# Layer 0: 148 score tiles of the maximum pass between the units of the expert network

## The reference, cut to what matters

```python
# layer 0, attention: 16 heads of 8, no causal mask
energy = einsum('bhqd,bhkd->bhqk', q, k) + bias_table[clip(pos_q - pos_k + N - 1, 0, 248)]
att = softmax(energy / (sqrt(C) * temp)); out = einsum('bhqk,bhkd->bhqd', att, v) @ Wp + bp
# layer 0, expert network: 2 shared and 8 routed experts, top 2 of 8, hidden size 256
ffn(x, w1, w2, w3) = (silu(x @ w1.T) * (x @ w3.T)) @ w2.T
out = sum over shared experts + sum over routed experts of combine[token, e] * ffn(x, expert e)
```

## Time and profile before

| | |
|---|---|
| runs | 1248.26, 1248.76, 1249.85 us |
| span of the profiled execution | 1246.1 us, on the only core |
| what lies around the span, against the median | 2.7 us |
| busy: TensorE, VectorE, ScalarE, GpSimd | 88%, 65%, 52%, 16% of the span |
| mean granted TensorE clock | 0.919 |

### The profile page before, as it was taken

The page is one execution under the profiler, slowest core; times in us unless marked ns, Lnnn a source line. Parts: engine busy times, 40 slices in busy tenths (PEclk is TensorE's granted clock), DMA queues, the critical chain, the costliest instruction groups (busy, mean ns, idle before and its releaser), DMA issues.

```text
span 1246.1 us, 19644 instructions
## 1 busy us (share of the span) xinstructions
PE 1097.0 (88%) x7308; PEld 516.1 (41%) x7308; DVE 815.6 (65%) x1631; ACT 648.9 (52%) x1257; POOL 193.2 (16%) x313
## 2 busy tenths in 40 slices
PE   6499999789999999999994589899999999897777
PEld 4366666322222222222232244434444467553444
DVE  5633333488998998898257678787876156546654
ACT  4323323217777787787742227566777533433434
POOL 2135555000100111011100001112221000001000
PEclk9699999859999999999987559889999999998888
DMA  4612213311112111010005302211233020000331
GB/s 117 218 47 93 93 60 96 103 28 27 46 49 51 43 37 45 16 39 12 19 1 178 98 21 76 64 56 47 85 105 122 18 77 1 1 1 0 137 136 34
DMA packets 62470, 77.79 MB, mean 62 GB/s; under 512 B 15836, under 2 KB 40108, under 8 KB 60588
## 3 DMA queue, kind: packets, MB, share of 16 engines
q1 hardware_dynamic: 53592, 65.34, 16.7%
q10 hardware_dynamic: 8788, 11.26, 3.1%
HBM read 61.32 MB, written 14.61 MB: 61 GB/s over the span
## 4 chain that ended last, share of the span: by engine, by line
PE 65%; DVE 20%; ACT 7%; SPq 3%; issue 3%; DMA 2%; ACTq 0%; POOL 0%; DVEq 0%
PE PS L1673 63%; DVE mx L1442 10%; ACT arena L943 5%; SPq L587 2%; SPq L595 1%; DMA arena<-drev_dram 1%; PE PS L1686 1%; DVE arena L1241 1%; DVE arena L1647 1%; DVE arena L1244 1%; DMA arena<-mrow 0%; DVE arena L1205 0%; DVE arena L1193 0%; DMA arena<-in_L_attn_x 0%; DVE small L1633 0%
## 5 line engine op out<-in xcount | busy, mean ns | idle before, releaser
L1673 PE MATMUL PS<-arena 128*32 128x512 f32 (+13 forms) x3656 | 606.4, 479 | 70.7 <-DVE mx L1442 20.7
L1442 DVE TENSOR_REDUCE mx<-PS 128x1 f32<-128x512 f32 (+3 forms) x896 | 500.5, 624 | 95.5 <-PE PS L1673 94.9
L943 ACT ACTIVATE arena<-PS 128x512 f32<-128x512 f32 (+3 forms) x896 | 438.3, 556 | 230.3 <-PE PS L1673 223.1
L1673 PEld LDWEIGHTS PS<-arena 128*32 128x32 f32 (+3 forms) x3656 | 159.0, 104 | 439.2 <-DVE mx L1442 175.2
L1673 PE MATMUL PS<-x_hi,w_hi_lo 128*128 128x512 f32 x320 | 145.1, 495 | 0.8 <-DVE combT L1305 0.4
L1548 DVE TENSOR_TENSOR fw<-PS,fw 128x512 f32<-128x512 f32 x80 | 55.3, 692 | 119.7 <-ACT fw L1002 117.9
L1002 ACT ACTIVATE fw<-PS 128x512 f32<-128x512 f32 x80 | 47.8, 597 | 123.5 <-PE PS L1673 123.5
L867 POOL TENSOR_TENSOR fw<-fw,arena 128x512 f32<-128x512 f32 x64 | 84.9, 1327 | 88.8 <-DVE fw L1548 88.8
L1673 PE MATMUL PS<-fw 128*128 128x512 f32 (+3 forms) x184 | 90.3, 578 | 0.0
L819 POOL TENSOR_TENSOR arena<-arena,fw 128x512 f32<-128x512 f32 x31 | 40.0, 1290 | 275.6 <-DMA fw<-sum_dram 275.6
L1673 PEld LDWEIGHTS PS<-x_hi,w_hi_lo 128*128 128x128 f32 x320 | 61.2, 191 | 31.1 <-issue 19.4
(11 more groups left out here) (313 smaller groups left out, 1113.9 us busy)
## 6 DMA issues: line engine op xcount, KB each, us to landing
arena<-comb_dram SPq DMA_DIRECT2D x14, 1024.0 KB, 5.0
arena<-comb_dram SPq DMA_DIRECT2D x18, 512.0 KB, 7.3
fw<-sum_dram SPq DMA_DIRECT2D x31, 256.0 KB
q_dram<-arena SPq DMA_DIRECT2D x24, 256.0 KB, 3.7
k_dram<-arena SPq DMA_DIRECT2D x24, 256.0 KB, 3.9
arena<-drev_dram SPq DMA_DIRECT2D x32, 192.0 KB, 4.3
arena<-k_dram ACTq DMA_DIRECT2D x20, 204.0 KB
fw<-in_ffn_w SPq DMA_DIRECT2D x10, 384.0 KB, 3.2
```

The source lines that it names most:

```text
L943: s.activation(Pr[:, m % 8, 0:w], bank(4 + m % 3, 0, w), ACT.Exp).then_inc(A["e_done"], 1)
L1442: v.reduce_max(mx[:, H % 2, kh, n:n + 1], bank(U % RING, 0, w), axis=AX.X, negate=True).then_inc(A["ring_free"], 1)
L1673: return nc.tensor.matmul(out_, lhsT, rhs, start=start, stop=stop)
```

## The change

`s_plan` puts 148 S units ahead of the main pass, and 26 (`SCORES_A_HALF`) on each of halves 0 to 13; halves 14 and 15 carry none. `lead_parts` cuts the 148: the first ten expert units have none, then each of the other 70 has one pair of S units, and the last 8 S units stand in four parts behind. TensorE's order in a part is: the w1 product, the pair of S units, the w3 product, the w2 product of three units before. The w1 product has bank 2 for itself and the w3 product bank 3, instead of two banks each, and the ring of S units has two banks (0 and 1) until the lead is over, and then four. The loops over experts are written out.

Around that: a low part of w1 and w3 is made on GpSimd, not VectorE; `dfull` and `dpart` are computed early, while VectorE waits for the first products of q; the choice of the experts is cut in pieces between the first four units, which no longer wait for it; six stores of bias rows instead of twelve (they are the same for both batches); each head group has its own `Hst` tile, loaded once; Q and K of batch 1 take the places of batch 0; SyncE stores q and k of batch 0, loads group 0, then group 1, and stores batch 1 after that, and takes weights and gate rows in step with the parts; the work of SyncE and GpSimd for the end of a half is placed at given steps.

```diff
-RING = 4
+RING, LEAD_RING = 4, 2
+UNITS = 2 * FFN_SEQ * NC
+FFN_LAG = 3
+LEAD_FROM, LEAD_REST = 10, 8
+LEAD_SCORES = 2 * (UNITS - LEAD_FROM) + LEAD_REST
+SCORES_A_HALF = 26
...
     if layer == 0:
-        return ends[H] + 20
+        upto = min(LEAD_SCORES + SCORES_A_HALF * H, KT * HG * 2 * HALVES // 2)
+        return [n for n, what in enumerate(stream) if what[0] == "S"][upto - 1] + 1
...
+def lead_parts(first):
+    parts, n = [[] for _ in range(LEAD_FROM)] + [[]], 0
+    for what in first:
+        if what[0] == "S" and n == 2:
+            parts.append([])
+            n = 0
+        n += what[0] == "S"
+        parts[-1].append(what)
+    return parts
...
+def ring_banks(layer, first, count):
+    lead = sum(what[0] != "K" for what in first) if layer == 0 else 0
+    banks = [U % (LEAD_RING if U < lead else RING) for U in range(count)]
+    before = [max((V for V in range(U) if banks[V] == banks[U]), default=None) for U in range(count)]
+    return banks, before
...
 # VectorE, attention(0)
-                    sequence(first_units[l])
+                    for n, part in enumerate(lead):
+                        sequence(part)
+                        if 4 <= n < UNITS:
+                            ffn_unit(n)
...
+            def ffn_unit(k):
+                dve.wait_ge(h3_ps, k + 1)
+                dve.wait_ge(a_made, k + 1)
+                if k >= 4:
+                    dve.wait_ge(y_done, k - 3)
+                v.tensor_tensor(fu[:, k % 4, :], bank(3), ft[:, k % 2, :], ALU.mult).then_inc(u_made, 1)
+            gate_first(0)
+            ffn_unit(0)
+            gate_second(0)
+            ffn_unit(1)
+            gate_shift(0)
+            ffn_unit(2)
+            gate_weights(0)
+            ffn_unit(3)
+            gate_out(0)
...
 # TensorE, attention(0)
+                    for n, part in enumerate(lead):
+                        if n == 4:
+                            comb_T(0, 1)
+                        if n == LEAD_FROM:
+                            pe.wait_ge(cb_ev, 1)
+                        if n < UNITS:
+                            gate_product(n)
+                        for what in part:
+                            ring_unit(what)
+                        if n < UNITS:
+                            linear_product(n)
+                        if FFN_LAG <= n < UNITS + FFN_LAG:
+                            down_product(n - FFN_LAG)
+                    pe.wait_ge(y_ev, NC)
...
+            def gate_product(k):
+                if k % (2 * NC) == 0:
+                    pe.wait_ge(wlo_made, expert_of(k) + 1)
+                if k < 2 * NC:
+                    pe.wait_ge(xlo_made, part_of(k) + 1)
+                if k:
+                    pe.wait_ge(a_made, k)
+                split_mm(bank(2), ...).then_inc(h1_ps, 1)
+            def linear_product(k):
+                if k:
+                    pe.wait_ge(u_made, k)
+                split_mm(bank(3), ...).then_inc(h3_ps, 1)
...
 # SyncE
+            store_qk(sp, 0, 0)
+            ...                       (six stores of bias rows, group 0, its bias tile, combT)
+            load_gate(0)
+            load_gate(1)
+            sp.wait_ge(att[0]["ld0"], 64)
+            load_group(sp, 0, 1)
+            load_bias(1)
+            store_qk(sp, 0, 1)
+            first_feed()              (expert weights, gate rows, maxima, sums, in step with the parts)
```

More of the change, by code:

```diff
@@ L160, in s_plan @@
         for what in part:
-            while i < len(steps) - 1 and done * t_total * (0.6 if layer == 0 and H == HALVES - 2 else 1.0) >= total * t_done and not (layer == 0 and second_of_pair(what)):
+            while i < len(steps) - 1 and done * t_total >= total * t_done and not (layer == 0 and second_of_pair(what)):
                 i += 1
@@ L424, in block_net @@
             for l in range(2)]
[L425 removed]
+        h_ld = [sem(f"h_ld{s}") for s in range(NG)]
         rw_in = [sem(f"rw_in{e}") for e in range(EXP)]
@@ L446, in block_net, with expert_of, routed, gated_before @@
             n_units.append(count)
+            banks, before = ring_banks(l, first_part, count)
+            ring_bank.append(banks)
+            ring_before.append(before)
+        lead = lead_parts(first_units[0])
+        assert len(lead) == UNITS + LEAD_REST // 2 and all(len(part) > 0 for part in lead[LEAD_FROM:])
+        def expert_of(k):
+            return k // (2 * NC)
+        def routed(k):
+            return 1 <= expert_of(k) <= EXP
+        def gated_before(k):
+            return k - 2 * NC
+        def part_of(k):
+            return k % (2 * NC) // 2
         def steps_before(l, H):
@@ L930, in attention @@
                     loads[-1]()
+                if l == 0:
+                    for k in range(2, UNITS):
+                        gate_half(k)
+                    act.wait_ge(y_done, UNITS)
+                    for c in range(NC):
+                        s.activation(n1T[:, chunk(c)], bank(4 + c), ACT.Silu).then_inc(y_ev, 1)
                 for H in range(HALVES):
@@ L1745, in s_adds @@
                                 rows = slice(64 - 64 * half, P - 64 * half) if (part, half) != (PARTS - 1, 1) else slice(0, P)
-                                pieces.append((dst[rows, h0:512], flip_of(row, half)[:, rows], Hst[row:row + 64, G % 2, pr, PARTS * half + part, 0:512 - h0]))
+                                pieces.append((dst[rows, h0:512], flip_of(row, half)[:, rows], Hst[G % NG][row:row + 64, pr, PARTS * half + part, 0:512 - h0]))
                         return pieces
```

480 lines of the change are left out of this document (231 added, 249 removed).

## The result

| | before | after | ratio, 95% interval |
|---|---|---|---|
| 20 runs each, median | 1249.53 us | 1243.03 us | 0.9934 [0.9911, 0.9956] |
| 12 more runs of the changed kernel (`again`), 20 of before beside them | 1247.14 us | 1240.09 us | 0.9942 [0.9917, 0.9968] |
| end of layer 0 in the profile (last evacuation) | 640.75 us | 632.00 us | |

The kernel is faster, by some 0.6%: the medians lie 6.5 and 7.1 us apart, and by the ratios it is 8.2 and 7.2 us. 1222 was predicted. The first profiled execution of the changed kernel was a disturbed one (1257.44 us), so every row here comes from the profile of `again`, the same kernel (1238.81 us, span 1237.0). Before, the profiled execution had a span of 1246.1 us.

What follows compares the result with a forecast made beforehand. VectorE, 89% busy in main-pass halves 1 to 13, was taken as the bound, beside a 2.42 us step loop. Start of main pass 0, main pass -26.5: 1248.8 - 26.5 = 1222.3 us; range 1203 to 1243, 8 in 10.

Steps and rivals of the forecast that it cites:

- step 1: Ahead of the units: `dfull` early, units 0 to 3 done by `combT`; part 10 begins at 65.5 us, bounds 63 to 68.
- step 2: Expert network: 70 parts with a pair at 2.77 us, 193.9, plus bias products 3.7, M 1.2, last S units 4.9, Silus 1.3.
- step 3: SyncE's queue: expert 2's weights asked for at about 69, wanted about 71; one wait of 2.5 us, bounds 0 to 6.
- step 4: Main pass: fewer S units a half; halves 1 to 13 -21.6 us, half 0 -4.7, half 14 -0.2; sum -26.5, bounds -34 to -17.
- the end of the DMA wait for bias tiles: Sign of being right: the 14.00 us DMA wait for bias tiles ahead of the main pass is gone.
- Rival A: TensorE limits both stages: parts 2.99 us (+15.4), main pass gains 17 instead of 26.5; 1247.2 us; chance 0.16, whole or half.
- halves above 21.5: Sign of the rival with TensorE as limit: main-pass halves still above 21.5 us with few waits on TensorE.
- B: Waits at seams of the parts: part 3.24 us, +33, total 1255 us, w3 products waiting for VectorE's product; chance 0.10.
- D: Late weight or gate row at every expert, 3 us at each of 8: +24, 1246 us, no change; chance 0.04.
- without idle time before it: Half 0 of the main pass, with its own bias tiles and no idle time before: 23.8 us instead of 28.5, -4.7.
- no gain and no loss up to here: Main pass begins at 273.0 us against 273.02 before, with 96 more tiles done by then.
- the margin of 0.7 us on VectorE: In each part, 0.7 us left before the w3 product would wait for VectorE's product and hold up TensorE.

Runs made afterwards that it cites:

- queue52: seams148 with batch 1's stores and later groups' tiles behind weights in SyncE's queue, and 52 S units ahead, 32 a half: 1220.07 us, ratio 0.9777.
- queue148: seams148 with batch 1's stores and later groups' tiles behind weights in SyncE's queue, still 148 S units ahead, 26 a half: 1225.10 us, ratio 0.9815.
- weights_early: The changed kernel with expert 2's w1 and w3 weights asked for ahead of gate rows, group 1 and batch 1's stores: 1232.47 us, ratio 0.9857.
- seams148: weights_early with M behind its part's w3 product and each Silu of the sum waiting only for its chunk's last w2 product: 1227.08 us, ratio 0.9821.
- seams140: seams148 with no S units behind the last expert unit, 140 ahead of the main pass and 27 a half: 1225.92 us, ratio 0.9819.

## Why the prediction was wrong, by its own steps

| term | forecast, us | `again`, us | difference |
|---|---|---|---|
| step 1: part 10 begins | 65.5 | 66.15 | +0.7 |
| step 2: 70 parts at 2.77 | 193.9 | 193.9 | 0 |
| step 2: bias products | 3.7 | 4.5 | +0.8 |
| step 2: four M products | 1.2 | 4.4 | +3.2 |
| step 2: last 8 S units, Silus | 6.2 | 7.5, what remains | +1.3 |
| step 3: weights of expert 2 | 2.5 | 9.9 | +7.4 |
| main pass begins | 273.0 | 286.34 | +13.3 |
| step 4: half 0 | 23.8 | 27.05 | +3.3 |
| step 4: halves 1 to 13 | 268.6 | 269.97 | +1.4 |
| half 14 | 20.1 | 19.96 | -0.2 |
| end of layer 0 | 614.25 | 632.00 | +17.75 |

**Right:** the price of a part, 2.77 us, the end of the DMA wait for bias tiles, layer 1 untouched. The halves are right as a time and in part by luck: step 4 put all of its 21.6 us down to six tiles fewer (1.66 a half), and the tiles gave 15.1 (1.16 a half); 5.2 came from edits that the sum had at nothing. Rival A (both stages limited by TensorE) is out in the parts, 2.77 and not 2.99. In the main pass its price, 1.3 us for six tiles, was nearer to the 1.16 than mine, though its sign (halves above 21.5) did not come: from 32 to 26 tiles TensorE's busy time in these halves falls by 17.1 us (270.10 to 252.98, `queue52` and `queue148`) and the span by 15.1. B is out, since no w3 product waits for VectorE; D is out in its form, since there was one late weight and not one at every expert.

**The step that failed is step 3.** I saw the queue, its order and the Silu behind the wait, and mis-sized it: 2.5 us, bound 6, where 9.9 stood. My "about 69" for the weights was 10 us early. `combT` was stored at 53.62 where I had 50: 3.6. The stores were priced from the earlier trace rows and took 10.4 for 9.5: 0.9. What was left between, 69 - 50 - 9.5 = 9.5 us, had to hold gate rows, group 1 and its bias tiles, none of them with a term or a row of its own, and it took 14.9, 9.72 of it the issue of the bias tiles: 5.4. `weights_early` shows the cost of the whole.

**Step 2 and step 4, two smaller ones of one kind.** I priced M as a product with tile changes and didn't ask on what it waits in a ring of two banks: 3.2 us, of which `seams148` gets 2.9 back. And half 0 was counted "without idle time before it", while my own sum had the Silus between the last w2 product and the first st. Of its 3.3 us, 1.8 are the low clock (25.8 from the first exponential where `seams148` has 24.0) and 1.3 the table load between the first st at 286.34 and the first exponential at 287.60, which step 2 had already counted ahead of the main pass.

**What the sum read rightly and the text wrongly.** I wrote "no gain and no loss up to here" of the start of the main pass, and that the 96 tiles bring the 26.5. The terms were near, but they mix two edits: the stage between the two vanished (with what stands around it a gain of 28 us, `queue52`), and 96 tiles moved (a loss of 2.6 us in the profile, `queue148` against `queue52`, and of some 9 by the estimate above, without the wait in half 14). By my own prices a pair of moved tiles costs 0.53 in a part; I never set that against what two tiles less give a half, and the medians of `queue148` and `queue52` lie 5 us apart, though not by more than their intervals allow.

With the late weights, M and the Silus mended and nothing else, `seams148` ends layer 0 at 616.00 against the forecast's 614.25, and its median is 22.0 us under before where 26.5 were forecast. The step that I had as the risk, the margin of 0.7 us on VectorE, cost nothing; the ones that cost were single waits at the ends of a long regular stretch. My range ended at 1243 because it was made of the bounds of steps 1, 2 and 4; step 3 stood in it with nothing, and its own bound was 6 us where 9.9 came.

## What to carry to other kernels

Price the issues of a queue one by one, from rows of the same transfer while the DMA engines are as busy as they will be, and put the load that an in-order engine waits for ahead of whatever is long to issue. Here a regular part could be forecast to the hundredth from three rows, and what was lost was lost at what happens once (the first part, the last, the odd unit in a short ring); so ask of each such instruction what it waits for and what is queued behind it. That a stage comes out at the forecast time doesn't show that the reason was right: change the one thing that the reason names, and see whether the time follows. When work moves from one stage to another, set the price per piece there against the price per piece here, and compare sizes only after looking in each variant's trace for a wait that the others don't have.

## What the runs showed of the hardware that was not expected

- The same four DMA issues from SyncE took 2.63 us in the kernel before and 6.11, 9.72 and 6.88 us in three places of `again`. At 9.72 the 16 DMA engines were busy (share 1.01, 280 GB/s in 57 to 67). That busy engines hold the issue back fits, but no run took the load away alone, so the cause stays open.
- A change from 128-row products to 64-row ones and back costs 0.31 us; with it, two S units side by side (0.53) are dearer than two whole-array products in a row (0.46).
- A wait of 1.45 us on TensorE, after w2 products and pairs, went with a granted clock of 0.76 to 0.78 over the next 15 us (half 0 1.9 us longer); with no wait it was 1.00. In `seams140` a wait of 0.69 us went with 0.83.
